# A state space block and a gated feed-forward part: dt projected first, and two queues re-ordered around it

## Chip, cores and metric

The kernel runs on one core of one Trainium2 chip. The metric is the device time of one execution in microseconds. The kernel before has a median of 790.67 us over three runs (789.48 to 793.22).

## The reference

Two sequences of 1024 tokens, width 512. First a Mamba-2 style mixer: layer norm, projection to 2368 columns (z 1024, x 1024, B 128, C 128, dt 64), a causal convolution with 4 taps over x, B and C and a silu, a scan over the tokens, gating by silu(z), an RMS norm, and the output projection, added to the input. Then a layer norm and a gated feed-forward part of 1408 columns, added again. All in float32.

```python
proj = hidden_states @ W_in * mup_vector
z, xBC, dt = jnp.split(proj, [D_SSM, D_SSM + CONV_DIM], axis=-1)
conv = conv_b + sum((conv_w[:, k] * xp[:, k:k + L] for k in range(K)))
dt = jax.nn.softplus(dt + dt_bias).reshape(B, L, G, Hg)
dA = jnp.exp(dt * (-jnp.exp(A_log)).reshape(G, Hg))
...
state = state * dA_t[..., None, None] + (dt_t[..., None] * x_t)[..., None] * B_t[:, :, None, None, :]
y_t = jnp.einsum('bghps,bgs->bghp', state, C_t)
...
g = y * jax.nn.silu(z)
g = g * jax.lax.rsqrt(jnp.mean(jnp.square(g), axis=-1, keepdims=True) + EPS) * norm_w
out = g @ W_out
```

## The kernel before

The mixer goes over 8 blocks of 128 tokens of both sequences (i = 0 to 7), each of 2 steps of 64 tokens (c = 2i and 2i + 1). Within a step the scan is written as products of matrices: a decay matrix of 64 x 64 per head, times C B^T, times x, plus a carry from the state. 64 heads stand in 4 groups of 16, and `ring` holds the decay matrix of one group in each of its 4 places. Weights and activations are split into a high and a low part, so that a product is three matmuls.

Each engine has a queue written out by hand in its own `body(i, first, last)`, and semaphores order the queues among each other. There is no planner: what stands behind a waiting instruction in a queue waits too.

TensorE (`body`, L1357): `turn_tok` and `turn_x` transpose B and x of a step, `carry` (L1279) is C times the state, `group` (L1299) the masked product of one head group into `ps_y`, `update` (L1312) one half of the state's update, `turn_xn` (L1217) turns the normalised input of the next block, `project(j, e)` (L1225) is event e of 10 of the input projection (event 0 is dt alone, with one tile of columns, events 1 to 9 two tiles), `project_out` the output projection of a step in two halves, `sum_squares` the sum for the RMS norm. `project` of events 0 and 1 waits for the low half of xn (`xn_split`); a later one for the evacuation two events before. `turn_xn` waits for the evacuations of events 8 and 9 of the running block, whose PSUM tiles it takes over.

ScalarE (`body`, L751): `evacuate` (L635) takes a projection out of PSUM; for event 0 these are four small instructions, a table load, an exp and a copy (L642 to L649), which start the polynomial for the logarithm in softplus. `clamp` (L712) and `fade` (L717) make the decay matrix of one group: relu, then exp. `gate_hi` is the high part of the gated y, `square` (L734) its square, `keep_tok` copies B's transpose, `norm_hi` the high part of xn, `make_run` three exps of the cumulated dt.

VectorE (`body`, L1038): `soft` (L917) is one of 11 steps of the logarithm's polynomial, on `dt_p` and `dt_e`, both in SBUF; `make_dt`, `make_d` and `make_cum` follow it. `mix` (L996) multiplies one group's decay matrix with C B^T, which lies in PSUM. `conv_taps` (L948) are 6 instructions for two tiles, with both inputs in SBUF. `update_state` (L1003) adds an update from PSUM to the state. `make_xpad` (L979) multiplies x by dt, `scale_carry` (L989) scales the carry, `gate_lo` is the low part of the gated y, `norm_lo` that of xn, `make_x1` (L1029) adds the output of two steps earlier to the residual, `make_y` and `gate` finish y in PSUM; `make_y` waits for all four groups.

GpSimd (`body`, L578): after the square of a step, `fold_squares` (L551, three instructions), `make_xw` (L532) and `fade_state` (L541), all on SBUF; then `diff` (L524) for the four groups of the next step, each behind a DMA that loads the ring.

SyncE issues the DMAs: ring loads from the cumulated dt in DRAM (two per group and step), residual rows, x1 stores, copies and checks of the expert weights.

Of the kernel before, what the change touches and what calls it, by code (L numbers as in the profile page):

```python
# [162 lines left out]
def mixer_phase(nc, x, w_in, w_out, packed, cum_dram, whole_dram, x1_dram, mlp_packed, down_s, hand, second):  # L163
    with ExitStack() as ctx:
# [451 lines left out]
        def _(act):  # L616
# [86 lines left out]
            def keep_tok(c):  # L703
                act.wait_ge(tok_turned, c + 1)
                act.activation(tok[:], ps_tok[:, 0:P], ACT.Copy).then_inc(tok_kept, 1)
# [45 lines left out]
            def body(i, first, last):  # L751
# [26 lines left out]
                if first:  # L778
                    weight_hi(EVENTS + 1)
                    norm_hi(i + 1, 0)  # L780
                    norm_hi(i + 1, 1)
                    for n in range(EVENTS + 2, PIECES):
                        weight_hi(n)
                    act.wait_ge(lo_made, LANDED_SKIP)
                    make_skip(i, 0)
                else:
                    mean_square(c - 1, 1)
                clamp(c + 1, 0)
                clamp(c + 1, 1)
                if not (first or last):  # L790
                    norm_hi(i + 1, 0)
                    norm_hi(i + 1, 1)
                if first:
                    evacuate(i + 1, 0)
                    gate_hi(c)
                    keep_tok(c + 1)
                else:
                    keep_tok(c + 1)
                    gate_hi(c)
                    if not last:  # L800
                        evacuate(i + 1, 0)

                c = STEPS * i + 1
                fade(c, 0)
                if last:
                    clamp(c, 2)
                    square(c - 1)
                else:
                    square(c - 1)
                    evacuate(i + 1, 1)  # L810
                    clamp(c, 2)
                fade(c, 1)
                clamp(c, 3)
                fade(c, 2)
                if not last:
# [68 lines left out]
        def _(dve):  # L884
# [153 lines left out]
            def body(i, first, last):  # L1038
# [67 lines left out]
                    return  # L1106
                mask_cb(c)
                make_xpad(i, 1)
                gate_lo(c - 1)
                if not first:  # L1110
                    make_x1(c - 2)
                for n in range(1, 4):
                    soft(i + 1, n)
                mix(c, 0)
                scale_carry(i, 1)
                for g in range(1, GROUPS):
                    mix(c, g)
                for n in range(4, LOGN):
                    soft(i + 1, n)
                make_dt(i + 1)  # L1120
                make_d(i + 1)
                make_cum(i + 1)
                conv_taps(i + 1, CONV_ORDER[0:2])
                conv_taps(i + 1, CONV_ORDER[2:4])
                update_state(c, 0)
                conv_taps(i + 1, CONV_ORDER[4:6])
                conv_taps(i + 1, CONV_ORDER[6:8])
                conv_taps(i + 1, CONV_ORDER[8:10])
# [87 lines left out]
        def _(pe):  # L1216
# [140 lines left out]
            def body(i, first, last):  # L1357
# [18 lines left out]
                if first:  # L1376
                    group(c, 2)
                    turn_xn(i + 1, 0)
                    turn_xn(i + 1, 1)
                    update(c, 1)  # L1380
                    group(c, 3)
                else:
                    sum_squares(c - 1)
                    update(c, 1)
                    group(c, 2)
                    group(c, 3)
                    if not last:
                        turn_xn(i + 1, 0)
                        turn_xn(i + 1, 1)
                turn_tok(i, 1)  # L1390
                turn_x(i, 1)
                if not first:
                    project_out(c - 1, SECOND_HALF)
                if last:
                    mlp_turn(0)
                    mlp_turn(1)
                else:
                    project(i + 1, 0)
                    project(i + 1, 1)

                c = STEPS * i + 1
# [398 lines left out]
```

## Time and profile before

| | us |
|---|---|
| median of three runs | 790.67 |
| the profiled execution's own time | 791.89 |
| its span | 790.1 |
| TensorE busy | 736.7 (93%) |
| VectorE busy | 526.2 (67%) |
| ScalarE busy | 492.1 (62%) |
| GpSimd busy | 293.8 (37%) |

The mean granted clock of TensorE is 0.986. Block 0 and what lies ahead of it take the first 112.28 us (to the carry of block 1), blocks 1 to 6 the time to 489.04, block 7 to about 535.6, and the feed-forward part the rest. Busy time of a matmul is counted to its modelled end, and matmuls overlap, so that 93% is not 93% of the peak. A timeline row gives the start, the duration, the engine, the line, the operation, output and input, how many instructions are merged, and in brackets the idle time before it with what ended it.

### The profile page before, as it was taken

What the parts mean: (1) busy time and instruction counts of PE and PEld (TensorE: products, weight loads), DVE (VectorE), ACT (ScalarE), POOL (GpSimd) and SP (SyncE); (2) the same over time, 40 slices, a digit from 0 to 9 for tenths busy, and PEclk for the clock granted to TensorE, in tenths of its full rate; (3) what the DMA queues carried; (4) which work ended last, traced back from release to release, by engine and by line L of the source; (5) the groups of instructions that cost most, each with busy time, mean ns of one, the idle gap of its engine ahead of it and who ended that gap; (6) DMA issues with size and microseconds to landing.
All of it is one profiled execution on the core that took longest, in us unless ns stands there. A gap on an engine that the chain in (4) does not pass through costs nothing.

```text
span 790.1 us, 20312 instructions
## 1 busy us (share of the span) xinstructions
PE 736.7 (93%) x8486; PEld 609.0 (77%) x8486; DVE 526.2 (67%) x845; ACT 492.1 (62%) x933; POOL 293.8 (37%) x235
## 2 busy tenths in 40 slices
PE   4886999999989999999999999889999999999997
PEld 4864887877877886787877887668888888888886
DVE  5968976887787797698698688683532532532331
ACT  5988987976977977878788797643322321321330
POOL 2173374466446626618618537450011011001002
PEclk9978999999999999999999999999999999999999
DMA  9823144484386256455545458665213003002002
GB/s 292 227 69 106 32 115 122 72 242 128 79 189 184 77 144 197 113 136 182 161 103 182 124 153 256 179 203 160 67 41 120 0 27 132 1 13 94 0 1 83
DMA packets 42299, 94.97 MB, mean 120 GB/s; under 512 B 9888, under 2 KB 15776, under 8 KB 42016
## 3 DMA queue, kind: packets, MB, share of 16 engines
q1 hardware_dynamic: 42208, 93.67, 41.7%
q8 instruction: 67, 1.10, 0.6%
q14 instruction: 24, 0.20, 0.1%
HBM read 84.73 MB, written 17.57 MB: 129 GB/s over the span
## 4 chain that ended last, share of the span: by engine, by line
PE 51%; DVE 22%; ACT 18%; issue 4%; DMA 2%; POOL 1%; SPq 1%; DVEq 0%; ACTq 0%; POOLq 0%
PE ps_y L1695 10%; PE ps_proj L1682 9%; DVE cx L945 9%; PE ps_out L1682 6%; PE ps_x L1682 6%; ACT ring L719 4%; ACT ring L715 4%; DVE dt_p L920 3%; PE ps_y L1308 3%; PE ps_proj L1236 2%; DVE state L1010 2%; PE ps_proj L1237 2%; PE ps_out L1332 2%; PE ps_proj L1238 2%; PE ps_x L1319 2%
## 5 line engine op out<-in xcount | busy, mean ns | idle before, releaser
L530 POOL TENSOR_TENSOR ring<-tokd,ring 128x1024 f32<-128x1024 f32 x64 | 122.6, 1927 | 188.8 <-ACT tokd L710 122.9
L1236 PE MATMUL ps_proj<-xn_hi,win_x_hi 128*128 128x256 f32 x352 | 101.8, 289 | 3.1 <-DVE xn_lo L914 3.1
L1237 PE MATMUL ps_proj<-xn_lo,win_x_hi 128*128 128x256 f32 x352 | 99.9, 284 | 0.0
L1238 PE MATMUL ps_proj<-xn_hi,win_x_lo 128*128 128x256 f32 x352 | 99.6, 283 | 0.0
L945 DVE SCALAR_TENSOR_TENSOR cx<-cin,consts,cx 128x256 f32<-128x256 f32 x240 | 96.3, 478 | 0.0
L1000 DVE TENSOR_TENSOR ring<-ring,ps_tok 128x1024 f32<-128x1024 f32 x64 | 77.1, 1218 | 20.7 <-ACT ring L719 20.6
L1551 POOL TENSOR_TENSOR res<-res,hidden 128x512 f32<-128x512 f32 (+1 forms) x16 | 20.1, 1257 | 166.3 <-DVE hidden L1614 160.6
L1236 PEld LDWEIGHTS ps_proj<-xn_hi,win_x_hi 128*128 128x128 f32 x352 | 67.3, 191 | 15.9 <-issue 11.4
L715 ACT ACTIVATE ring<-ring 128x1024 f32<-128x1024 f32 x64 | 66.7, 1058 | 19.3 <-POOL ring L530 19.3
L1236 PE MATMUL ps_proj<-xn_hi,win_z_hi 128*128 128x256 f32 x256 | 74.5, 291 | 0.0
L1237 PE MATMUL ps_proj<-xn_lo,win_z_hi 128*128 128x256 f32 x256 | 72.8, 284 | 1.5 <-issue 1.5
L1238 PE MATMUL ps_proj<-xn_hi,win_z_lo 128*128 128x256 f32 x256 | 72.7, 284 | 0.0
L1237 PEld LDWEIGHTS ps_proj<-xn_lo,win_x_hi 128*128 128x128 f32 x352 | 67.4, 192 | 0.2
L1238 PEld LDWEIGHTS ps_proj<-xn_hi,win_x_lo 128*128 128x128 f32 x352 | 67.4, 191 | 0.0
L719 ACT ACTIVATE ring<-ring 128x1024 f32<-128x1024 f32 x64 | 66.6, 1054 | 0.1
L1695 PE MATMUL ps_y<-wd,h_hi 128*128 128x512 f32 x165 | 65.8, 399 | 0.0
L1695 PE MATMUL ps_y<-wd,h_lo 128*128 128x512 f32 x165 | 65.0, 394 | 0.0
L1572 ACT ACTIVATE silu_g<-ps_out,scales 128x512 f32<-128x512 f32 x24 | 16.5, 688 | 68.1 <-PE ps_x L1682 68.0
L1308 PEld LDWEIGHTS ps_y<-ring,xpad 64*32 64x32 f32 x4096 | 43.7, 107 | 19.2 <-issue 14.9
L1308 PE MATMUL ps_y<-ring,xpad 64*32 64x64 f32 x4096 | 49.8, 229 | 5.0 <-DVE ring L1000 2.6
L1332 PE MATMUL ps_out<-wout_hi,g_hi 128*128 128x512 f32 x120 | 49.7, 414 | 3.8 <-DVE res L1035 3.8
L1574 ACT ACTIVATE h_hi<-hidden 128x512 fp32r<-128x512 f32 x44 | 27.8, 632 | 40.6 <-DVE hidden L1639 40.6
(186 smaller groups left out, 1897.0 us busy)
## 6 DMA issues: line engine op xcount, KB each, us to landing
ring<-cum_dram SPq DMA_DIRECT2D x128, 256.0 KB, 4.7
xin<-x SPq DMA_DIRECT2D x8, 512.0 KB, 3.7
res<-x SPq DMA_DIRECT2D x32, 128.0 KB, 2.6
x_dram<-res SPq DMA_DIRECT2D x32, 128.0 KB, 2.7
res<-x_dram SPq DMA_DIRECT2D x16, 256.0 KB, 2.7
out<-res SPq DMA_DIRECT2D x15, 256.0 KB, 2.1
x_in_sb<-x_dram SPq DMA_DIRECT2D x3, 1024.0 KB, 6.0
gate_w_copy<-gate_w SPq DMA_DIRECT2D x4, 704.0 KB, 5.7
```

The lines of the kernel that those rows point to most:

```text
L530: pool.tensor_tensor(ring[:, g, :, :], own, ring[:, g, :, :], ALU.subtract).then_inc(diffed, 1)
L715: act.activation(ring[:, g, :, :], ring[:, g, :, :], ACT.Relu).then_inc(clamped, 1)
L719: act.activation(ring[:, g, :, :], ring[:, g, :, :], ACT.Exp, scale=-1.0).then_inc(faded, 1)
L945: dve.scalar_tensor_tensor(cx[:, m, :, :], cin[:, m, :, k:k + Q], col(C_CW + 4 * m + k), cx[:, m, :, :], ALU.mult, ALU.add).then_inc(tap_m ...
L1000: dve.tensor_tensor(ring[:, g, :, :], ring[:, g, :, :], ps_cb.unsqueeze(1).to_broadcast([P, GH, Q]), ALU.mult).then_inc(mixed, 1)
L1236: pe.matmul(out, hi[:, k, :], xn_hi[:, k, :], start=(k == 0), stop=False)
L1237: pe.matmul(out, hi[:, k, :], xn_lo[:, k, :], start=False, stop=False)
L1238: made = pe.matmul(out, lo[:, k, :], xn_hi[:, k, :], start=False, stop=(k == KT - 1))
L1308: made = pe.matmul(ps_y[32 * pair:32 * pair + 32, at:at + Q], xpad[half(b), g * GH + h, :], ring[half(b), g, h, :], start=(c == g == n == ...
L1332: pe.matmul(out_of(c), hi[:, k, :], wout_hi[:, k, :], start=(k == 0), stop=False)
L1682: made = pe.matmul(out_ps, a, b, start=(k == 0 and x is xn_hi), stop=(k == KT - 1 and x is xn_lo))
L1695: made = pe.matmul(ps_o[t % 2], a, b, start=(m == 0 and h is h_hi), stop=(m == MT - 1 and h is h_lo))
```

## The change

The order of the entries in three engines' queues is changed; no instruction is added or taken away.

TensorE: `turn_xn` of the next block goes ahead of groups 2 and 3 of the first step, and `project(i + 1, 0)` (dt) ahead of the second half of `project_out`, which then stands between projections 0 and 1. In the last block that half goes ahead of `turn_tok`. ScalarE: `norm_hi` goes ahead of the two clamps of the second step, `keep_tok` ahead of the evacuation of dt in block 0 too, `gate_hi` behind the evacuation of dt and the first fade, `clamp(c, 2)` and `fade(c, 1)` ahead of evacuation 1, and the square behind it. VectorE: logarithm steps 1 to 3 go ahead of `make_x1` and `gate_lo`, steps 4 to 7 between masking products 1 and 2, 8 to 11 behind 3; the first half of the state's sum goes ahead of the second pair of conv tiles.

```diff
@@ scalar, body: first step's end
                     mean_square(c - 1, 1)
+                    if not last:
+                        norm_hi(i + 1, 0)
+                        norm_hi(i + 1, 1)
                 clamp(c + 1, 0)
                 clamp(c + 1, 1)
-                if not (first or last):
-                    norm_hi(i + 1, 0)
-                    norm_hi(i + 1, 1)
-                if first:
+                keep_tok(c + 1)
+                if last:
+                    gate_hi(c)
+                else:
                     evacuate(i + 1, 0)
-                    gate_hi(c)
-                    keep_tok(c + 1)
-                else:
-                    keep_tok(c + 1)
-                    gate_hi(c)
-                    if not last:
-                        evacuate(i + 1, 0)
 
                 c = STEPS * i + 1
                 fade(c, 0)
+                if not last:
+                    gate_hi(c - 1)
+                clamp(c, 2)
                 if last:
-                    clamp(c, 2)
                     square(c - 1)
-                else:
+                fade(c, 1)
+                if not last:
+                    evacuate(i + 1, 1)
                     square(c - 1)
-                    evacuate(i + 1, 1)
-                    clamp(c, 2)
-                fade(c, 1)
                 clamp(c, 3)
@@ vector, body: second step
                 make_xpad(i, 1)
-                gate_lo(c - 1)
-                if not first:
-                    make_x1(c - 2)
                 for n in range(1, 4):
                     soft(i + 1, n)
                 mix(c, 0)
+                if not first:
+                    make_x1(c - 2)
+                gate_lo(c - 1)
                 scale_carry(i, 1)
-                for g in range(1, GROUPS):
-                    mix(c, g)
-                for n in range(4, LOGN):
+                mix(c, 1)
+                for n in range(4, 8):
+                    soft(i + 1, n)
+                mix(c, 2)
+                mix(c, 3)
+                for n in range(8, LOGN):
                     soft(i + 1, n)
                 make_dt(i + 1)
                 make_d(i + 1)
                 make_cum(i + 1)
                 conv_taps(i + 1, CONV_ORDER[0:2])
+                update_state(c, 0)
                 conv_taps(i + 1, CONV_ORDER[2:4])
-                update_state(c, 0)
@@ tensor, body: first step's end
                     update(c, 1)
-                    group(c, 2)
-                    group(c, 3)
                     if not last:
                         turn_xn(i + 1, 0)
                         turn_xn(i + 1, 1)
+                    group(c, 2)
+                    group(c, 3)
+                if last:
+                    project_out(c - 1, SECOND_HALF)
                 turn_tok(i, 1)
                 turn_x(i, 1)
-                if not first:
-                    project_out(c - 1, SECOND_HALF)
...
                     project(i + 1, 0)
+                    if not first:
+                        project_out(c - 1, SECOND_HALF)
                     project(i + 1, 1)
```

## Rows read from the trace of the kernel before

**Rows 1.** Busy time of each engine by stretch, a block in each

```profile
core 0: us, PE busy (x) PEld busy (x) DVE busy (x) ACT busy (x) POOL busy (x), PEclk, DMA share, GB/s
...
112.28:174.44 62.16, 59.30 (x922) 49.55 (x922) 50.66 (x83) 51.29 (x103) 33.52 (x24) 1.00 0.55 133
...
237.60:299.91 62.31, 59.45 (x923) 49.66 (x923) 51.46 (x84) 51.29 (x103) 33.54 (x24) 1.00 0.51 143
299.91:363.83 63.92, 59.58 (x922) 49.48 (x922) 51.44 (x84) 51.16 (x103) 33.54 (x24) 1.00 0.50 142
...
426.09:489.04 62.95, 59.74 (x923) 49.70 (x923) 51.48 (x84) 51.30 (x103) 33.58 (x24) 1.00 0.57 162
```

**Rows 2.** Waits of TensorE: total us, times, longest

```profile
PE ps_x L1285 <- DVE xpad L986: 11.8, 7, 3.8
PE ps_x L1319 <- DVE state L1010: 6.1, 5, 1.3
```

**Rows 3.** Timeline of TensorE, block 3: start us, duration us

```profile
251.90 1.09 PE L1222 MATMUL ps_proj<-eye,xin 128*128 128x128 f32 x8
...
254.14 0.48 PE L1332 MATMUL ps_out<-wout_hi,g_hi 128*128 128x512 f32 x1
...
256.98 0.28 PE L1236 MATMUL ps_proj<-xn_hi,win_x_hi 128*128 128x256 f32 x1
261.34 1.94 PE L1285 MATMUL ps_x<-state,cx 128*64 128x512 f32 x8
...
299.91 1.51 PE L1285 MATMUL ps_x<-state,cx 128*64 128x512 f32 x6 [1.62 <-DVE xpad L986]
```

**Rows 4.** Timeline of VectorE, block 3

```profile
252.00 1.23 DVE L1015 TENSOR_TENSOR ps_y<-ps_y,skip 128x1024 f32<-128x1024 f32 x1 [0.18 <-PE ps_y L1308]
...
255.45 1.29 DVE L914 TENSOR_TENSOR xn_lo<-ps_proj,xn_hi 128x512 fp32r<-128x512 f32 x2 [0.94 <-ACT xn_hi L632]
...
262.48 0.94 DVE L920 SCALAR_TENSOR_TENSOR dt_p<-dt_p,dt_e 128x128 f32<-128x128 f32 x3 [1.76 <-ACT dt_p L649]
...
276.25 4.82 DVE L945 SCALAR_TENSOR_TENSOR cx<-cin,consts,cx 128x256 f32<-128x256 f32 x12
...
291.64 1.23 DVE L1021 TENSOR_TENSOR ps_y<-ps_y,sz 128x1024 f32<-128x1024 f32 x1
```

**Rows 5.** Timeline of TensorE, block 4

```profile
320.81 0.38 PE L1236 MATMUL ps_proj<-xn_hi,win_x_hi 128*128 128x256 f32 x1 [1.50 <-DVE xn_lo L914]
```

**Rows 6.** Timeline of ScalarE, block 3

```profile
258.61 0.92 ACT L642 ACTIVATE dt_e<-ps_proj,consts 64x128 f32<-64x128 f32 x2 [0.34 <-PE ps_proj L1238]
...
263.41 1.03 ACT L739 ACTIVATE sq<-ps_y 128x1024 f32<-128x1024 f32 x1
```

**Rows 7.** Timeline of GpSimd, block 3

```profile
264.52 2.65 POOL L556 TENSOR_TENSOR sq<-sq 128x512 f32<-128x512 f32 x3 [3.37 <-ACT sq L739]
...
269.02 3.77 POOL L548 TENSOR_TENSOR state<-state,whole 128x2048 f32<-128x2048 f32 x1
```

**Rows 8.** Logarithm step and masking product: timeline; min/median/max ns of each line

```profile
271.80 1.14 DVE L920 SCALAR_TENSOR_TENSOR dt_p<-dt_p,dt_e 128x128 f32<-128x128 f32 x1
...
L920 DVE SCALAR_TENSOR_TENSOR dt_p<-dt_p,dt_e x88: 281/292/1156, 18.4 to 464.1; 128x128 f32<-128x128 f32 x88
...
L1000 DVE TENSOR_TENSOR ring<-ring,ps_tok x64: 1207/1220/1223, 46.8 to 518.4; 128x1024 f32<-128x1024 f32 x64
```

**Rows 9.** Timeline of TensorE and VectorE, block 0

```profile
40.01 1.11 PE L1276 MATMUL ps_x<-eye,cx 128*128 128x128 f32 x8 [2.56 <-ACT cx L697]
...
74.69 3.32 PE L1285 MATMUL ps_x<-state,cx 128*64 128x512 f32 x8 [3.80 <-DVE xpad L986]
...
88.62 1.65 DVE L945 SCALAR_TENSOR_TENSOR cx<-cin,consts,cx 128x256 f32<-128x256 f32 x4
```

**Rows 10.** Stretches behind idle time of TensorE, with its granted clock (PEclk)

```profile
40.97:44.38 3.41, 3.41 (x19) 3.41 (x18) 0.46 (x2) 3.39 (x5) 3.41 (x3) 0.50 0.02 5
...
75.10:78.50 3.40, 3.40 (x10) 1.05 (x7) 3.03 (x6) 2.71 (x5) 1.53 (x2) 0.50 0.00 0
```

## The prediction

> All stages are told in the clock of block 3 of the profiled execution, 237.60 to 299.91 us, the cleanest block [rows 1]; 0.5% of 790.67 is 4.0 us, about what a measurement can tell from no change.
>
> **What bounds the kernel now.** First the table by stretches [rows 1]: the mixer's six inner blocks take 62.16 to 63.92 us each, of which TensorE is busy 59.3 to 60.3, VectorE and ScalarE some 51. So TensorE has only about 2.9 us of slack per block, and the shared expert part behind 535.6 is TensorE alone; nothing in the diff touches that. Then the waits of TensorE [rows 2]: the carry product waits for the expanded x (7 times, 11.8 us), the second state update waits for the state's sum (5 times, 6.1 us). Then the timelines of block 3. From the carry at 237.60 to the second carry at 261.34 TensorE issues without a gap [rows 3]; VectorE waits for it. After that the roles turn: VectorE runs logarithm steps, masking products, softplus, conv taps, state sums, y and gate with few pauses until 292.87 [rows 4, 6], and the next carry at 299.91 comes 1.62 us after TensorE was ready [rows 3]. Thus a block is two halves in series: TensorE up to y, VectorE from the logarithm to the gate. An edit that delays VectorE's half delays the block by as much; one that speeds it up gains at most what TensorE had to wait.
>
> **TensorE's edits.** No product is added. (a) The eight transposes of xn (0.93 us, 251.90 to 252.83) go ahead of groups 2 and 3, whose end releases y. They need the evacuation of tile 9, which ScalarE's queue has done by then, and a normalised xn, there too at 250.48. So y starts at 252.93 instead of 252.00, the gate at 254.20, and the low half of xn at 255.35. Before, that low half stood waiting 0.94 us for ScalarE [rows 4]; now ScalarE has the high half early. It ends at 256.65, as before. (b) The dt projection now follows turn_x directly. TensorE is there at 254.14 + 0.24, but needs the low half: it idles 2.3 us until 256.70, where the second half of project_out used to stand. Then 12 products 1.5, project_out 2.84 (254.14 to 256.98), projection 1 2.85: carry at 263.95 instead of 261.34 [rows 3]. Alone that uses up 2.6 of the 2.9 us of slack: period 62.1. In block 4 the high half stood behind a clamp whose difference waited for a DMA, and TensorE lost 1.50 to the late low half [rows 5]; with the high half ahead of the clamps this loss goes.
>
> **ScalarE and the logarithm.** dt's evacuation starts 1.7 after the projection: 258.43 instead of 258.61, first logarithm step at 262.29 instead of 262.48 [rows 4, 6]. The fade of group 0 is at 262.1, gate_hi at 263.1, clamp 2 at 264.0, fade 1 at 265.0, evacuation 1 at 265.95, and only then the square, at 266.65 (it needs gate_lo anyway; these by the 1.0 us of such an instruction, [rows 6]). Before, the square ran at 263.41. It ends at 267.65, 3.2 us later, and GpSimd's three instructions, which start at 264.52 and end at 272.79 now [rows 7], follow it: folds 2.65, xw 1.9, fading of the state 3.77.
>
> **VectorE among GpSimd's work: the step that decides.** The logarithm steps read two tensors of SBUF. In the trace the first of the eight behind mix 3 took 1.14 us, from 271.80 to 272.94, where 0.29 is the median; the fading of the state ended at 272.79. The maximum over all 88 is 1.156 [rows 7, 8]. A masking product beside the same instruction stays at 1.22 (64 of them between 1.207 and 1.223) [rows 8]; it reads one operand from PSUM. So I read: a logarithm step waits until GpSimd's running instruction is over, and a masking product does not. What that makes of the new order: soft 1 to 3 262.29, mix 0 263.2, x1 264.4, gate_lo 265.0, scale_carry 266.15 (the carry ends at 265.9), mix 1 267.3 to 268.45. Soft 4 meets the first fold (267.7 to 269.0) and ends at 269.3. The second fold had waited for it and runs to 269.95; soft 5 ends at 270.25, the third fold at 270.7, soft 6 at 271.0, xw at 272.9, soft 7 at 273.2, and the fading of the state runs to 277.0. Mix 2 and mix 3 pass beside it, 273.2 to 275.5. Soft 8 waits until 277.0, soft 9 to 11 end at 278.2, dt, d and the scan take 1.0: the conv starts at 279.2, against 276.25 [rows 4]. That is +2.95 us, where without any waiting it would be 275.05, a gain of 1.2. The price of the waits is 4.1 per block: 0.6 + 0.7 + 0.45 + 1.9 + 1.5, less the 0.85 that 275.05 still contains.
>
> From the nearest rows: the measured wait is 0.85 once per block; five waits of such a size would be 4.2. The lower bound is 0 (steps slip between), the upper one 4.1 + 2.5, when soft 7 comes behind the fading instead of xw. I take 4.1, because ScalarE's queue fixes the square and GpSimd's three follow it without a pause.
>
> The Trainium skill says the same in general: SBUF — State Buffer, section "Who interferes with whom": a VectorE instruction with two SBUF inputs and a GpSimd instruction that reads SBUF exclude each other for a whole instruction, whoever starts first. The trace agrees for the step at 271.80. By this rule GpSimd's folds would wait for steps as well, as I assumed; were it one-sided, the conv would start about 1 us sooner.
>
> **State's sum two taps sooner.** Six conv instructions (2.4 us) earlier: it ends at 282.7 by the new clock, and TensorE reaches its second update at 283.5. The 1.23 us wait of [rows 2] goes, but TensorE is not the late one in this half any more. Conv, sum, y and gate then end 2.9 later, ScalarE's and VectorE's tail to the carry is unchanged: 299.91 + 2.95 = 302.86. TensorE would be ready at 298.29 + 2.61 - 1.24 = 299.66 and idles 3.2 us.
>
> **Clock.** TensorE fell to a granted clock of 0.50 (1.2 of 2.4 GHz) after idles of 2.56 and 3.80 us [rows 9, 10], and stayed at 1.00 after 1.62 and 1.50 [rows 1, 3, 5]. At the low clock the carry took 3.32 instead of 1.94 [rows 3, 9]; with what follows I take 1.5 per fall. The 3.2 us idle before the carry should cause it nearly always: five of six blocks, 7.5 us, all on the path since TensorE leads there. The new 2.3 us idle before the dt projection lies between the rows. I take two of six. There it delays the second carry by 1.3 and lets soft 7 meet the fading: 2.5 each, 5.0. Bounds: 0 and 6 x 2.5 = 15.
>
> The Trainium skill, TensorE: Matmul & The Clock Gate, section "Why this matters for your kernels", asks only that gaps stay under about 3 us. The trace has a fall after 2.56, so it does not hold here. By the page the sum would be 5 us less.
>
> **Block 0.** Keep_tok moves ahead of the dt evacuation, so the 3.80 us wait of the carry [rows 9] shrinks to 1.0, and TensorE gains 2.8 and the clock. But VectorE, reckoned as above: soft 4 at 77.5, folds and xw interleaved to 83.0, the fading to 86.8, conv at 89.05 against 88.62. Next carry 112.7 against 112.28 [rows 1, 9]: +0.4, the gain is lost.
>
> **Block 7** has no logarithm; its long wait is for a ring load behind the x1 store, which hides a late clock: 0.
>
> **Sum** against the profiled execution's own 791.89 (span 790.1 and 1.8 around it). Six blocks at 65.26, 391.6, and 1.2 of TensorE's fetch pauses in the first halves, less 489.04 - 112.28 = 376.76 [rows 1]: +16.0 (block 4's loss is gone in it). Block 0 +0.4. Clock +7.5 and +5.0. Together +28.9: 820.8. The median of the three runs stands 1.2 below the profiled one: 819.6.
>
> **Rivals.**
> (A) The waits come, but TensorE's clock holds through the new idles: +16.4, 807. For it: the falls of the trace are few. Against: 2.56 was enough.
> (B) Soft 7 falls behind the fading in every block (mix 1 only 0.6 us later than reckoned does it): 6 x 2.5 more instead of the second clock term, 16.4 + 15 + 7.5 = 38.9, 829.6.
> (C) The other side: logarithm steps are not held, or slip between GpSimd's instructions. Then the conv starts at 275.05, the carry is possible at 299.05 and TensorE, ready at 299.7, decides: 0.2 gained per block, 1.5 in block 4, 3.8 in block 0 (carry at 108.5, no idle long enough for the clock), 6.5 in all; three falls behind the 2.3 us idle give back 4.5. 788.7. It decides from the point where the waits sum to less than 1 us per block. Against: the 1.14 is in every block with the same end.
> (D) As (C) with no fall of the clock, 784.2. Needs both; the 2.56 row speaks against.
>
> **Chances.** Main 0.57, (A) 0.17, (B) 0.13, (C) 0.07, (D) 0.04; the rest is for things unseen. Range 804 to 832: from just under (A) to above (B). Faster by over 0.5% 0.06, within 0.06, slower 0.88.
>
> **What would show it.** Right: L920 with many durations of 0.5 to 3 us and a first conv tap 41 to 44 us behind the block's carry (38.65 now); the square about 29 to 30 behind it (25.8 now); L1319's wait for L1010 gone; the wait of L1285 near 3.2 per block; a wait of L1236 for L914 of 2.3 in each block; granted clock under 1.00 in the inner blocks. Wrong: L920 at 0.29 throughout, blocks of 62, and gains in block 0.

## The result, and the profile after

The changed kernel takes 818.44 us, median of four runs (813.02 to 820.89), where the kernel before takes 790.51 in the same session: ratio 1.034 [1.028, 1.040], slower. The profiled execution took 819.64, its span is 817.9, the mean granted clock 0.968 (0.986 before).

The page of the changed kernel, its busy table and TensorE's clock in 40 slices:

```profile
span 817.9 us, 20312 instructions
PE 752.8 (92%) x8486; PEld 621.9 (76%) x8486; DVE 550.3 (67%) x845; ACT 493.8 (60%) x933; POOL 294.0 (36%) x235
PEclk9998999998999999999989999999999999999999
```

VectorE has 24 us more of busy time and TensorE 16 with the same instructions; GpSimd has 0.2 more. The table by blocks answers to [rows 1] (us; busy time of the engines; clock; DMA share; GB/s):

```profile
0.00:111.50 111.50, 86.99 (x1113) 76.54 (x1113) 91.11 (x151) 91.76 (x180) 43.06 (x44) 0.95 0.52 144
111.50:176.56 65.06, 61.21 (x923) 50.95 (x923) 52.96 (x83) 51.40 (x103) 33.66 (x24) 0.97 0.52 127
176.56:247.42 70.86, 64.15 (x923) 53.48 (x923) 56.62 (x85) 52.80 (x104) 34.55 (x26) 0.93 0.50 129
247.42:313.57 66.15, 61.44 (x923) 51.13 (x923) 53.30 (x83) 50.18 (x102) 32.76 (x23) 0.97 0.48 133
313.57:379.33 65.76, 61.43 (x922) 51.16 (x922) 54.34 (x84) 51.43 (x103) 33.62 (x24) 0.97 0.45 137
379.33:450.09 70.76, 66.96 (x922) 54.14 (x922) 56.97 (x85) 52.42 (x104) 35.21 (x27) 0.90 0.50 145
450.09:515.73 65.64, 60.01 (x924) 49.66 (x923) 53.73 (x83) 50.72 (x102) 32.16 (x22) 1.00 0.52 152
```

Blocks 1 to 6 take 404.23 us, against 376.76: +27.5. Four blocks stand at 65.1 to 66.2, two at 70.8. The forecast had 65.26 for a block before its two clock terms, and 67.3 on the average with them (65.26 and a sixth of 12.5); the average measured is 67.4. Block 0 is 0.8 shorter, block 7 1.1 longer (47.67 against 46.56); the feed-forward part has its 254.50 in both. The sum is the 27.8 us between the spans.

Where in a block the time goes is seen when it is cut at its second carry. The means over blocks 1 to 6, in us, from the starts of the carries in the traces; the two lower kernels are experiments that are told further down:

| kernel | first carry to second | second carry to the next block |
|---|---|---|
| before | 24.2 | 38.6 |
| changed | 28.6 | 38.7 |
| changed, output projection first | 24.8 | 40.9 |
| changed, without the second step's fading | 28.2 | 36.9 |

Nearly all of the loss, 26.5 of the 27.5 us, lies in TensorE's half. VectorE's half keeps its old length: what the new order gains in it, the steps' waits for GpSimd's fading take away again (without them it is 1.7 us shorter than before, of which 0.85 is a wait that the kernel before has too).

TensorE's waits after answer to [rows 2]: the carry's wait is a little smaller, the one for the state's sum is left in block 0 only, and a new one stands on top, for the low half of xn in front of the dt projection. Then the logarithm steps, all 88:

```profile
PE ps_proj L1236 <- DVE xn_lo L911: 15.1, 7, 2.3
PE ps_x L1285 <- DVE xpad L983: 10.0, 6, 2.1
...
PE ps_x L1319 <- DVE state L1004: 1.8, 1, 1.8
```

```profile
L917 DVE SCALAR_TENSOR_TENSOR dt_p<-dt_p,dt_e x88: 280/293/3736, 17.5 to 490.8; 128x128 f32<-128x128 f32 x88
```

The median of a step is 0.293 as in [rows 8], the longest 3.74 (1.16 before). Block 1, carry at 111.50, VectorE and GpSimd (start us, duration us):

```profile
141.29 1.23 DVE L990 TENSOR_TENSOR rows<-ps_x,tokd 128x1024 f32<-128x1024 f32 x1 [0.54 <-PE ps_x L1285]
142.43 1.21 DVE L997 TENSOR_TENSOR ring<-ring,ps_tok 128x1024 f32<-128x1024 f32 x1
143.56 3.56 DVE L917 SCALAR_TENSOR_TENSOR dt_p<-dt_p,dt_e 128x128 f32<-128x128 f32 x4
147.04 2.34 DVE L997 TENSOR_TENSOR ring<-ring,ps_tok 128x1024 f32<-128x1024 f32 x2
149.30 2.57 DVE L917 SCALAR_TENSOR_TENSOR dt_p<-dt_p,dt_e 128x128 f32<-128x128 f32 x4
...
152.90 1.25 DVE L942 SCALAR_TENSOR_TENSOR cx<-cin,consts,cx 128x256 f32<-128x256 f32 x3
```

```profile
142.37 2.66 POOL L556 TENSOR_TENSOR sq<-sq 128x512 f32<-128x512 f32 x3 [6.72 <-ACT sq L739]
144.98 1.99 POOL L539 TENSOR_TENSOR xw<-xpad,tokd 128x1024 f32<-128x1024 f32 x1
146.93 3.81 POOL L548 TENSOR_TENSOR state<-state,whole 128x2048 f32<-128x2048 f32 x1
```

Steps 4 to 7 take 3.56 us, where four that nothing holds take 1.26. Step 4 takes its 0.29; steps 5 to 7 take 0.75, 0.50 and 1.91, each about as long as the GpSimd instruction beside it (the second fold 0.74, the third 0.46, xw 1.99). Step 7 gets in as xw ends at 146.97, in front of the fading. Step 8 waits until the fading is over at 150.74; 9 to 11 follow freely. The masking products between them take their 1.2 us each. The conv starts 41.40 behind the carry, against 38.65 in [rows 4].

Block 2 is 5.8 us longer than block 1, and only a part of that is VectorE's. GpSimd started 0.47 us ahead of mix 1 (209.77, against 0.06 ahead in block 1), so that step 7 comes behind the start of the fading instead of in front of it:

```profile
210.24 1.21 DVE L997 TENSOR_TENSOR ring<-ring,ps_tok 128x1024 f32<-128x1024 f32 x1
211.37 6.92 DVE L917 SCALAR_TENSOR_TENSOR dt_p<-dt_p,dt_e 128x128 f32<-128x128 f32 x4
...
220.47 1.26 DVE L917 SCALAR_TENSOR_TENSOR dt_p<-dt_p,dt_e 128x128 f32<-128x128 f32 x4
...
222.76 0.46 DVE L942 SCALAR_TENSOR_TENSOR cx<-cin,consts,cx 128x256 f32<-128x256 f32 x1
```

```profile
214.33 3.81 POOL L548 TENSOR_TENSOR state<-state,whole 128x2048 f32<-128x2048 f32 x1
```

Four steps take 6.92, and mix 2 and mix 3 stand behind them; but steps 8 to 11 then find GpSimd idle and take 1.26 instead of 2.57. From mix 1 to the conv it is 12.5 us, against 10.5 in block 1: 2.0 us are the price of step 7's place. Another 2.7 stand in front, since the second carry comes 30.6 us behind the first instead of 27.8, after a stall of instruction issue (an idle of TensorE for which the trace shows no releaser) and a clock fall that lasts twice as long:

```profile
193.19 0.34 PE L1308 MATMUL ps_y<-ring,xpad 64*32 64x64 f32 x14 [1.48 <-issue]
```

The last 1.0 stands behind the conv, which starts 46.2 behind the carry. In block 5, the other long one, GpSimd was 0.29 ahead and the four took 7.10; from mix 1 to the conv it is 12.7 us, the second carry comes 29.4 behind the first, and 1.9 stand behind the conv. In blocks 3, 4 and 6 GpSimd started 0.2 to 0.6 us behind mix 1, and no step took over 1.91. Some of TensorE's idles of 1.6 us and more, at carries, a dt projection and behind stalls of instruction issue:

```profile
111.50 1.08 PE L1285 MATMUL ps_x<-state,cx 128*64 128x512 f32 x4 [2.10 <-DVE xpad L983]
176.56 0.65 PE L1285 MATMUL ps_x<-state,cx 128*64 128x512 f32 x2 [1.61 <-DVE xpad L983]
197.36 0.58 PE L1236 MATMUL ps_proj<-xn_hi,win_x_hi 128*128 128x256 f32 x1 [2.28 <-DVE xn_lo L911]
...
379.33 2.61 PE L1285 MATMUL ps_x<-state,cx 128*64 128x512 f32 x8 [2.10 <-DVE xpad L983]
421.38 1.86 PE L1319 MATMUL ps_x<-xw,tok 64*128 64x512 f32 x2 [1.71 <-issue]
```

In the inner blocks the granted clock fell eight times to 0.50 (1.2 of 2.4 GHz), six times for 3.4 us and twice for 6.8; two of the stretches:

```profile
196.50:200.00 3.50, 2.64 (x12) 2.64 (x13) 2.99 (x6) 0.00 (x0) 3.42 (x4) 0.50 0.14 47
...
421.50:428.20 6.70, 6.70 (x25) 5.20 (x25) 6.49 (x16) 2.98 (x9) 0.00 (x0) 0.50 0.10 23
```

Five of the eight begin in or right behind the new idle before the dt projection (blocks 1 to 5), one at a carry (379.33), two behind a stall of instruction issue (2.12 us before 236.71, 1.71 before 421.38).

### The profile page after: what moved, and what is told of

Same layout as the page of the kernel before. It is cut to its first block, busy times and chain, and to the rows that moved or that the text cites. A ratio compares the mean times of both kernels' runs of the same rounds, so it can differ in the third digit from the quotient of the medians.

```text
span 817.9 us, 20312 instructions
## 1 busy us (share of the span) xinstructions
PE 752.8 (92%) x8486; PEld 621.9 (76%) x8486; DVE 550.3 (67%) x845; ACT 493.8 (60%) x933; POOL 294.0 (36%) x235
## 4 chain that ended last, share of the span: by engine, by line
PE 68%; DVE 16%; ACT 7%; issue 5%; DMA 2%; SPq 1%; POOL 0%; DVEq 0%; ACTq 0%
PE ps_y L1697 9%; PE ps_proj L1684 9%; PE ps_proj L1236 5%; PE ps_out L1684 5%; PE ps_x L1684 5%; PE ps_proj L1237 5%; PE ps_proj L1238 5%; DVE cx L942 5%; PE ps_y L1308 4%; PE ps_out L1332 3%; PE ps_x L1285 3%; PE ps_x L1319 3%; PE ps_out L1333 3%; PE ps_out L1334 3%; DVE dt_p L917 2%
## 5 line engine op out<-in xcount | busy, mean ns | idle before, releaser
L1236 PE MATMUL ps_proj<-xn_hi,win_x_hi 128*128 128x256 f32 x352 | 105.4, 300 | 15.9 <-DVE xn_lo L911 15.1
L1237 PE MATMUL ps_proj<-xn_lo,win_x_hi 128*128 128x256 f32 x352 | 102.7, 292 | 0.0
L1238 PE MATMUL ps_proj<-xn_hi,win_x_lo 128*128 128x256 f32 x352 | 102.5, 291 | 0.0
L1236 PEld LDWEIGHTS ps_proj<-xn_hi,win_x_hi 128*128 128x128 f32 x352 | 70.0, 199 | 29.8 <-DVE xn_lo L911 14.8
L917 DVE SCALAR_TENSOR_TENSOR dt_p<-dt_p,dt_e 128x128 f32<-128x128 f32 x88 | 57.9, 658 | 30.9 <-ACT dt_p L649 28.7
L1237 PEld LDWEIGHTS ps_proj<-xn_lo,win_x_hi 128*128 128x128 f32 x352 | 70.4, 200 | 0.3
L1238 PEld LDWEIGHTS ps_proj<-xn_hi,win_x_lo 128*128 128x128 f32 x352 | 70.3, 200 | 0.0
L556 POOL TENSOR_TENSOR sq<-sq 128x512 f32<-128x512 f32 (+2 forms) x48 | 39.9, 831 | 53.8 <-ACT sq L739 51.3
L1332 PE MATMUL ps_out<-wout_hi,g_hi 128*128 128x512 f32 x120 | 52.6, 439 | 2.9 <-DVE res L1032 2.9
```

The lines of the kernel that those rows point to most:

```text
L917: dve.scalar_tensor_tensor(dt_p[:], dt_p[:], log_c[LOGN - 1 - n], dt_e[:], ALU.add, ALU.mult).then_inc(soft_step, 1)
L1236: pe.matmul(out, hi[:, k, :], xn_hi[:, k, :], start=(k == 0), stop=False)
L1237: pe.matmul(out, hi[:, k, :], xn_lo[:, k, :], start=False, stop=False)
L1238: made = pe.matmul(out, lo[:, k, :], xn_hi[:, k, :], start=False, stop=(k == KT - 1))
L1332: pe.matmul(out_of(c), hi[:, k, :], wout_hi[:, k, :], start=(k == 0), stop=False)
```

## The experiments

Each ratio is to the kernel before, in the same session; 1% is 7.9 us.

**The split of the steps alone.** The kernel before with only

```diff
-                for g in range(1, GROUPS):
-                    mix(c, g)
-                for n in range(4, LOGN):
-                    soft(i + 1, n)
+                mix(c, 1)
+                for n in range(4, 8):
+                    soft(i + 1, n)
+                mix(c, 2)
+                mix(c, 3)
+                for n in range(8, LOGN):
+                    soft(i + 1, n)
```

> The kernel before with one edit: logarithm steps 4 to 7 stand between masking products 1 and 2, steps 8 to 11 behind 3. Waiting theory (a step waits for GpSimd's running instruction): step 4 meets xw, step 5 the fading of the state until about 272.8 in block 3's clock, the conv starts near 278.3 instead of 276.25: about 2 us in each of seven blocks, and TensorE's wait before the carry grows to 3.6 us, so that its clock falls there in some: 804 to 811. Rival (steps are not held): the split only reorders 3.4 us of work, 790.

Measured 1.017 [1.012, 1.021]: 803.7 us on the scale of 790.5, just under the expected range. VectorE, block 3 of this kernel:

```profile
272.93 5.42 DVE L920 SCALAR_TENSOR_TENSOR dt_p<-dt_p,dt_e 128x128 f32<-128x128 f32 x4
...
```

The four steps in front take 5.42 us and hold up the masking products, which themselves would not have waited. That is the wait for GpSimd, called the lock from here on, at the price expected (the conv of block 3 starts 40.88 behind the carry, 2.2 later than before). TensorE's longer wait did not come at the carry (0.3 to 1.6 us there, 3.6 expected) but at the state's sum, and in four blocks its clock falls to 0.50 with that wait:

```profile
PE ps_x L1322 <- DVE state L1010: 17.5, 7, 3.1
```

**The split undone in the changed kernel** (the same edit backwards).

> The changed kernel with logarithm steps 4 to 11 all behind masking product 3 again. Waiting theory: what holds the conv is the end of GpSimd's fading, which follows the late square; eight steps instead of four then come behind it: about 1.3 later in the four ordinary blocks, 1 us earlier in the two in which step 7 met the fading: 818 to 824. Rival (the split is what costs): 803 to 808.

Measured 1.036 [1.032, 1.040], 819 us on the scale: no gain at all (the longest step is 3.79). With the square late, eight steps behind mix 3 meet the same fading. So the split is sufficient for a loss, but not needed for the one of the changed kernel. Blocks 2 and 5 are the long ones here too, though there is no step between mix 1 and mix 2:

```profile
181.49:251.68 70.19, 64.66 (x923) 52.83 (x923) 53.17 (x84) 51.57 (x103) 33.57 (x24) 0.93 0.48 128
...
386.41:457.01 70.60, 67.00 (x922) 54.09 (x922) 54.52 (x85) 52.36 (x104) 35.19 (x27) 0.90 0.49 144
```

In these two the low clock lasted 10.2 and 13.6 us, in block 1 3.4. The place of step 7 is thus the smaller part of what makes a block long.

**The late square alone.** The kernel before with ScalarE's gate_hi behind the first fade, the square behind the second, and VectorE's make_x1 and gate_lo behind mix 0:

```diff
@@ scalar
                 fade(c, 0)
+                if not last:
+                    gate_hi(c - 1)
+                clamp(c, 2)
                 if last:
-                    clamp(c, 2)
                     square(c - 1)
-                else:
+                fade(c, 1)
+                if not last:
+                    evacuate(i + 1, 1)
                     square(c - 1)
-                    evacuate(i + 1, 1)
-                    clamp(c, 2)
-                fade(c, 1)
...
```

> The kernel before with only ScalarE's and VectorE's order of the gated y changed: gate_hi behind the first exponential, the square behind the second, gate_lo behind mixing product 0. The steps stay in one run of eight, the output projection stays ahead of the dt projection. Theory: the square comes 3 to 3.5 us later, so GpSimd's folds, weighting and fading end near 276 in block 3 instead of 272.8; the eight steps start at 271.8, two or three pass before the fading, the rest wait for its end, and the convolution starts 2.0 to 2.8 us later. Six blocks at 2.4 and up to 4 us of clock falls at the carry: 804 to 810 us. Rival (only the split of the steps costs time): within 2 us of the kernel before.

Measured 1.027 [1.020, 1.034], 812 us on the same scale, above the expected range. VectorE and GpSimd, block 3:

```profile
282.34 6.05 DVE L921 SCALAR_TENSOR_TENSOR dt_p<-dt_p,dt_e 128x128 f32<-128x128 f32 x8
```

```profile
282.18 3.77 POOL L548 TENSOR_TENSOR state<-state,whole 128x2048 f32<-128x2048 f32 x1
```

The fading starts as the steps do, so that they wait for nearly the whole of it instead of two or three slipping by; the conv starts 42.1 to 43.6 behind the carry in six blocks, and TensorE waits 2.9 to 3.2 us for the state's sum in each, with a fall of the clock. Alone, this edit is the dearest part of the change.

**The dt projection first, alone.**

```diff
@@ scalar
                     keep_tok(c + 1)
-                    gate_hi(c)
-                    if not last:
+                    if last:
+                        gate_hi(c)
+                    else:
                         evacuate(i + 1, 0)
+                        gate_hi(c)
@@ tensor
-                if not first:
+                if last:
                     project_out(c - 1, SECOND_HALF)
-                if last:
                     mlp_turn(0)
                     mlp_turn(1)
                 else:
                     project(i + 1, 0)
+                    if not first:
+                        project_out(c - 1, SECOND_HALF)
                     project(i + 1, 1)
```

> The kernel before with the third part of the change alone: the dt projection ahead of the output projection's second half and, so that the exponentials are ready for it, ahead of gate_hi; gate_hi and the square stay ahead of the second exponential, the steps are not split. Theory: a 2.3 us wait for xn_lo in front of the dt products in six blocks and the clock falls behind it, less the exponentials that come 1 us sooner, and up to 1 us more for the square: 797 to 805 us, which with the late gate and the split alone shows that each of the three costs time by itself and that they don't add up. Rival (the wait only costs together with the late GpSimd): 789 to 793.

Measured 1.016 [1.009, 1.022]; TensorE waits for xn_lo:

```profile
PE ps_proj L1238 <- DVE xn_lo L916: 13.6, 7, 3.2
```

Split 1.7%, late square 2.7%, dt first 1.6% add up to 6.0%; the change as a whole costs 3.4%. What was expected held: each costs by itself, and they overlap.

**The projection's order undone, wholly and by half.** The changed kernel with all four tiles of project_out's second half back ahead of the dt projection, and with two of the four:

> The changed kernel with the second half of project_out ahead of the dt projection again, all else as changed. Waiting theory: TensorE's 2.2 us idle behind the transposes and the clock falls there go, but the conv still starts near 279, so TensorE waits 5 to 6 us before the carry and its clock falls there: 806 (no falls) to 815 (all). Rival (dt first is the main cost): 795 or less.

> The changed kernel with the first two of the four tiles of the output projection's second half ahead of the dt projection, the other two behind it. The 2.3 us wait for xn_lo would be filled by some 1.4 us of products, and 0.9 us are left. Theory (what costs is the idle and the clock falls behind it, and a wait under 1 us brings no fall): 6 x 1.4 us of idle becomes work and most falls go, 805 to 810 us, near the 808.4 of the kernel with all four tiles ahead. Rival (the time goes by the place of the dt projection alone, so each tile ahead of it delays the logarithm's chain by as much as it fills): 817 to 819.

Measured 1.021 [1.017, 1.024] and 1.018 [1.010, 1.025]. Two tiles do as much as four, within the noise. With two, the wait for xn_lo is 6.2 us in all instead of 15.1, the longest 1.5:

```profile
PE ps_proj L1236 <- DVE xn_lo L911: 6.2, 7, 1.5
```

and no fall of the clock begins behind it. With two tiles there are still three falls in the inner blocks, two with an idle of 2.10 at the carry and one with an issue stall of 2.94; with four there is one, at a carry. So 10 to 13 us (1.3 to 1.6%) of the change are the 2.3 us idle and what it brings: the falls behind it, and the later mix 1 that let step 7 meet the fading, for here no step takes over 1.91. The experiments do not separate these.

The wait of 5 to 6 us before the carry that was expected for four tiles came in pieces: 2.10 at most at the carry, and the rest in shorter waits for ScalarE and GpSimd, 4.1 to 4.7 us in all from the second carry to the next block.

```profile
PE ps_proj L1236 <- ACT cin L661: 5.6, 7, 0.8
...
PE ps_x L1319 <- POOL xw L539: 3.5, 7, 0.6
```

**GpSimd's fading taken out.** The changed kernel with the fading of the second step cut to 16 of 2048 columns (the state is left unfaded there):

```diff
+                if j == 1:
+                    s = state[:, 0, 0:HEAD]
+                    pool.tensor_tensor(s, s, whole[:, 0, j:j + 1].to_broadcast([P, HEAD]), ALU.mult).then_inc(state_faded, 1)
+                    return
```

> The changed kernel in which GpSimd fades only 16 of 2048 state columns in the second step of each block (part of the state's decay is left out). Waiting theory: no step can meet the 3.8 us instruction: the conv comes 1.3 us sooner in ordinary blocks and some 6 in the two long ones, all blocks near 64: 797 to 804. Rival (waits have another cause, GpSimd is off the path): 818.

Measured 1.014 [1.010, 1.017]. VectorE's program is that of the changed kernel, yet the longest step is down to one xw, and TensorE's wait for xpad to less than half:

```profile
L921 DVE SCALAR_TENSOR_TENSOR dt_p<-dt_p,dt_e x88: 278/293/1914, 17.3 to 474.0; 128x128 f32<-128x128 f32 x88
```

```profile
PE ps_x L1289 <- DVE xpad L987: 4.5, 6, 1.6
```

2.0% or 16 us go with this one GpSimd instruction. That is more than its part in the change, for the kernel before waits for its fading too (0.85 us in a block), and the kernel before without a fading was not run. Of the 17.5 us between the two profiled executions 3.6 lie in block 0, 5.2 and 3.3 in blocks 2 and 5, and 0.6 to 1.7 in each of the others. The 1.4% that are left fit the dt idle, which stays in this kernel with a fall of the clock in each of the six blocks.

**keep_tok and the norm's high half, alone** (on the kernel before).

> The kernel before with two of the changed kernel's moves alone: keep_tok ahead of the evacuation in block 0, and the norm's transposes ahead of groups 2 and 3 with norm_hi ahead of the clamps. Theory: the first move takes the 3.3 to 3.8 us wait of the carry at 74.69 and the clock fall behind it away, the second is covered everywhere else: 785 to 788 us. Rival (block 0 is ended by VectorE's chain to its convolution, which the carry's wait doesn't touch): 789.5 to 791.

Measured 0.997 [0.994, 1.000]. The carry of block 0 is at 71.05 without a wait instead of 74.69, and block 1 starts at 111.00 (112.28): 1.3 gained, not 3. Block 4 takes 62.35 instead of 63.92, as its wait for the low half is gone. But block 2 takes 64.67 (63.16) and block 3 63.31 (62.31), with longer issue stalls, so the last inner carry is at 490.09, 1.05 later than before. Both mechanisms are seen, the gain is not. (The profiled execution, at 794.22, is the slowest of the ten of this kernel.)

**Early steps.** If steps beside GpSimd cost, steps in its idle time should gain. The kernel before with

```diff
-                for n in range(1, 4):
+                for n in range(1, 7):
                     soft(i + 1, n)
                 mix(c, 0)
```

> The kernel before with logarithm steps 4 to 6 moved from behind the masking products to ahead of mixing product 0, where VectorE has work only from 263.42 and GpSimd none until 264.52 (block 3); steps 7 to 11 stay behind product 3. Theory (a step beside GpSimd's work waits for it, and the convolution's start sets the block): three steps of 0.29 us leave the stretch that ends in the convolution, so that it starts 0.9 us sooner after each carry, and the carries that they delay by 0.9 are covered by the 1.3 us idle before mixing product 1. Seven blocks at 0.9 give 6.1 us: 784 us where the kernel before is at 790.5 (range 782 to 787), and the first step behind product 3 still waits about 1 us for the fading. Rival (the steps' place costs nothing, only the number of instructions counts): 790.5, ratio 1.000.

Measured 0.995 [0.991, 0.998], 786 us on the scale of 790.5, some 4 us of the 6 expected. In all six inner blocks the conv starts 0.5 to 1.1 us sooner behind the carry. Part is given back in block 2, where TensorE stalls for 2.78 us, and the kernel before for 1.46 at the same product:

```profile
228.65 0.28 PE L1237 MATMUL ps_proj<-xn_lo,win_z_hi 128*128 128x256 f32 x1 [2.78 <-issue]
```

**GpSimd's work moved instead, VectorE untouched.**

```diff
+                    if j == 1 and not closing:
+                        make_xw(i, j)
                     if not opening:
                         fold_squares(c - 1)
-                    if not closing:
+                    if j == 0:
                         make_xw(i, j)
```

> The kernel before, VectorE's program untouched; on GpSimd alone the weighting xw (1.94 us, it waits for nothing at 261.15 in block 3) goes ahead of the folds in the second step of each block, into the 3.4 us that GpSimd is idle there. Its work then ends near 270.9 instead of 272.8. Theory (VectorE's steps wait for GpSimd's instruction in progress): the first step behind mixing product 3 no longer waits 0.85 us, the convolution starts 0.9 us sooner in most blocks, 0.5 us of it given back by step 1, which meets xw: 783 to 788 us. Rival (the steps wait for something else, or the end is set elsewhere): 789.5 to 791.5.

GpSimd and VectorE, block 3:

```profile
259.23 1.93 POOL L539 TENSOR_TENSOR xw<-xpad,tokd 128x1024 f32<-128x1024 f32 x1
262.74 2.65 POOL L556 TENSOR_TENSOR sq<-sq 128x512 f32<-128x512 f32 x3 [1.58 <-ACT sq L741]
265.35 3.79 POOL L548 TENSOR_TENSOR state<-state,whole 128x2048 f32<-128x2048 f32 x1
```

```profile
260.70 1.26 DVE L922 SCALAR_TENSOR_TENSOR dt_p<-dt_p,dt_e 128x128 f32<-128x128 f32 x3 [2.28 <-ACT dt_p L651]
270.02 2.57 DVE L922 SCALAR_TENSOR_TENSOR dt_p<-dt_p,dt_e 128x128 f32<-128x128 f32 x8
```

The eight steps take 2.57 instead of 3.43, and step 1 waits 0.3 for xw: the trace shows what was expected, and the profiled execution took 786.25. Over ten runs the ratio is 0.997 [0.994, 1.001], which can't be told from no change: the mechanism is shown here, a gain in time is not.

**Both, and with the harmless parts of the change.**

> The same with logarithm steps 4 to 6 ahead of mixing product 0 as well. Theory: GpSimd is done before mixing product 3 is, five steps are left behind it and none waits, so that the dt step comes at about 273.6 in block 3 (275.26 before, 274.53 with the early steps alone): 1.5 to 1.7 us in each of seven blocks, 779 to 783 us. Rival (GpSimd's end and the early steps relieve the same microsecond once): 785 to 788, as the early steps alone.

> The previous kernel with what the change does elsewhere and that cost nothing: keep_tok first in block 0, the norm's transposes and norm_hi sooner, the state's sum two taps sooner. Theory: 1 to 1.5 us less in block 0 and nothing in the others, since the 23.66 us from the convolution to the carry have been the same in every kernel, with and without the 1.2 us wait for the state: 778 to 782 us. Rival (the state's wait is on the path: six times 1.2 us more come off): 771 to 775.

Measured 0.995 [0.992, 0.998] and 0.997 [0.994, 1.000]. In the first, the conv comes 36.7 to 38.1 us behind the carry in five of six blocks (38.5 to 40.3 before), and this was lost again: in block 0 the six early steps meet the fading and take 7.86 us; in block 2 the clock falls twice, each time behind an issue stall (1.81 and 1.96 us of idle). In the second, the exponentials come sooner still, and in blocks 3 and 4 an early step runs into the fading (block 3, VectorE):

```profile
260.79 8.68 DVE L922 SCALAR_TENSOR_TENSOR dt_p<-dt_p,dt_e 128x128 f32<-128x128 f32 x6 [1.16 <-ACT dt_p L651]
```

The carry's scaling stands behind it, TensorE waits 4.32 us and its clock falls for 7 us (4.33 and 3.4 in block 4). For the first kernel the rival's time (785 to 788) is what came, 786 on the scale of 790.5, no better than the early steps alone; but not for its reason, as the conv did start sooner than with those. For the second the rival was wrong too: removing the state's wait brought nothing. The best kernels of the study stand half a percent below the kernel before, at the edge of what can be told.

## Why the prediction was right

Forecast 819.6 with 804 to 832, measured 818.44. That the mechanism was right is shown by the experiments; that the time is met within 1.2 us is in part luck, since terms that were off by several us made up for each other. Step by step:

- **The deciding step, steps beside GpSimd: right.** In the four even blocks the conv came 41.4 to 42.5 behind the carry, where 41.6 was worked out, and the square 29.75 to 30.9 behind it (29 to 30 was said); the steps took up to 3.7 us, and the masking products were unmoved. That the experiment without the fading gave back 16 us, as much as the sum's first term (+16.0), is chance: it takes more away than the change had added, and 3.6 of it are in block 0.
- **A slip in the working.** Without any wait the new order would bring the conv to about 274.3 and not 275.05: mix 1 ends at 268.45, and behind it stand eight steps, two masking products and 1.0 for the dt instructions. The waits are then 4.9 us and not 4.1. The forecast time does not hang on it, since 279.2 was worked out step by step.
- **Two errors that made up for each other.** The second carry was reckoned 26.35 behind the first and came at 27.8 in block 1, the clock having fallen in between. From there to the conv 15.25 was reckoned and 13.6 came. One reason is GpSimd: folds and xw were assumed to wait for the steps, 9.3 us from the first fold to the end of the fading. Its instructions took 2.66, 1.99 and 3.81 against 2.65, 1.94 and 3.77 of [rows 7], 8.4 us in all. A step of 0.29 us that got in between two of them held up the second by 0.05 us at most.
- **Who holds whom.** The Trainium skill (SBUF — State Buffer, "Who interferes with whom") lets either engine be the one that waits. The steps show only VectorE waiting, but the trace agrees with the page where VectorE's instruction is long: in block 0, before and after the change, xw took 2.91 us instead of 1.94 to 1.99. A VectorE instruction with two SBUF inputs, which takes 1.23 by itself, had waited for GpSimd's instruction before it, and now xw waited for that one:

```profile
43.94 2.05 DVE L886 TENSOR_TENSOR win_z_lo<-state,win_z_hi 128x1024 fp32r<-128x1024 f32 x1
44.87 2.91 POOL L539 TENSOR_TENSOR xw<-xpad,tokd 128x1024 f32<-128x1024 f32 x1
```

- **Rival (B)'s mechanism came in two of six blocks**, at 1.5 to 2 us each, where 2.5 was said. It had been priced as an all-or-nothing case and, in the clock term, as two blocks of six; in which blocks it comes is decided by GpSimd's start, 0.3 and 0.5 us ahead of mix 1 in the two, 0.06 ahead to 0.6 behind in the others. The rest of what makes these blocks 5 us longer than the others is issue stalls, on which the prediction has 1.2 us in all, and clock falls.
- **The clock: the number right by luck, the place wrong.** Seven falls were forecast, five at carries and two behind the dt idle; eight came: one, five, and two behind issue stalls. The carry waits 1.6 to 2.1 us in five of seven blocks and not at all behind the two long ones, where 3.2 was said for each: the fall behind the dt idle had already made TensorE 1.4 us late at the second carry. The dt idle with its falls costs 10 to 13 us by both experiments, against 5.0; the 7.5 for five falls at carries is too much by about as much, as one came.
- **The length of the idle does not decide a fall by itself.** The prediction placed 2.3 us between rows that stayed (1.50, 1.62) and rows that fell (2.56, 3.80). The later traces show both outcomes on either side: a fall after 1.50 in the kernel without the fading, none after 2.78 in the one with early steps (at 228.65, the row shown with that experiment).

```profile
406.75 1.53 PE L1323 MATMUL ps_x<-xw,tok 64*128 64x512 f32 x2 [1.50 <-issue]
407.20:410.50 3.30, 3.30 (x12) 2.29 (x11) 3.30 (x7) 2.74 (x9) 0.00 (x0) 0.50 0.15 28
...
228.65:232.05 3.40, 3.40 (x29) 3.40 (x29) 2.31 (x3) 2.22 (x4) 3.13 (x2) 1.00 0.94 227
```

- **The rule that gaps stay under about 3 us**, which the Trainium skill has (TensorE: Matmul & The Clock Gate, "Why this matters for your kernels"), was set aside on the 2.56 row; the trace bears that out, with falls after 2.23 (at 130.54 and 267.35) and 2.10.
- **Block 0** gained 0.8 where a loss of 0.4 was given: the carry at 70.61 has no wait at all. **Block 7** lost 1.1 where 0 was given; what in it costs that was not tried. The state's wait is gone as said, and brought nothing, here and in the last experiment.
- **Rivals (A), (C), (D)** fell: the clock does fall, eight times in the inner blocks, and steps are held.

What stays open: what sets the length of TensorE's issue stalls; what besides the length of an idle decides whether the clock falls, and what the falls cost apart from the idles before them; and in how many of the runs without a profile there are two long blocks.

## What to carry to other kernels

Before a short VectorE instruction with two SBUF inputs is moved "into a gap" between others, look at what GpSimd does in that gap: in this kernel a step of 0.29 us took up to 3.74, and all that stood behind it waited as well. An instruction off the critical path (here ScalarE's square, which starts GpSimd's chain) can be the one whose delay costs most: 2.7% when moved alone. Work that fills TensorE's wait for another engine can be worth more than its own time, since in this kernel an idle of 2.1 to 2.3 us before the dt projection was followed by half the clock for 3 to 7 us in five blocks of six; half of the filling work did as well as all of it.

## What the runs showed of the hardware

- The lock holds either engine, but not equally in this kernel: VectorE's steps took up to 3.79 us beside GpSimd's instruction, while the means of GpSimd's fading, xw and first fold in the changed kernel are 3.79, 2.02 and 1.29 us against 3.78, 2.00 and 1.28 before. One xw, of block 0, was held for 0.9 us by VectorE's subtraction of 128x1024 elements.
- An idle of 2.10 us before the carry brought a fall to 0.50 at 379.33, and none at 111.50; 1.61 and 1.85 (at 176.56 and 313.57) brought none, and 1.50 to 1.54 brought falls in two experiments. Stalls of instruction issue of 1.7 and 2.1 us were followed by falls as waits were, others of 2.4 and 2.8 were not.
- One issue stall stands at the same product of block 2 (projection by win_z with xn_lo) in twelve of the fourteen traces of this case, 1.04 to 2.94 us long, though the kernels differ in order alone (one of them in the length of the fading too). The two traces without it are those of the split alone and of the late square alone, where TensorE had waited 3.0 and 3.2 us for the state's sum shortly before.
- The kernel before ran between 787.1 and 798.9 us in 25 runs of one session. Gains of 0.9 us per block, plain in a trace, are of the size of one issue stall or one fall of the clock.
